# Middle periods: two turned blocks ahead of the first logits tile, its maximum behind one pass of the third sum, its exponential inside an attended tile

## The reference

```
for n in range(2):                       # STEPS
    q = Xa @ W1.T @ W2.T ; k = Xa @ W3.T
    probs  = softmax(q @ k.T)            # 2048 x 2048
    A      = probs, per row only the largest entries whose sum reaches 0.9 (top-p), renormalised
    Xf     = R @ Xf                      # R = row-normalised adj + I
    Xa     = A @ Xa
    Z      = Z + Xf @ U1[n].T + Xa @ U2[n].T
```

## Time and profile before

| | us |
|---|---|
| runs (3) | 1101.89 median, 1100.0 to 1106.16 |
| profiled execution | 1101.68 |
| its span, first to last instruction | 1099.9 |
| PE busy | 843.0 |
| DVE busy | 778.8 |
| ACT busy | 511.9 |
| POOL busy | 68.5 |
| mean granted TensorE clock | 0.890 of full speed |

### The profile page before, as it was taken

The page is one execution under the profiler, slowest core; times in us unless marked ns, Lnnn a source line. Parts: engine busy times, 40 slices in busy tenths (PEclk is TensorE's granted clock), DMA queues, the critical chain, the costliest instruction groups (busy, mean ns, idle before and its releaser), DMA issues.

```text
span 1099.9 us, 12251 instructions
## 1 busy us (share of the span) xinstructions
PE 843.0 (77%) x3886; PEld 568.4 (52%) x3886; DVE 778.8 (71%) x2357; ACT 511.9 (47%) x979; POOL 68.5 (6%) x66
## 2 busy tenths in 40 slices
PE   5889959853787778558778188688678899997695
PEld 5754326532565666456455065557575485543342
DVE  5968679799989989932788898798887102235715
ACT  4876245265466476223533835836743431123212
POOL 0120110000000000000000000000011100002201
PEclk9989988886998998979788599999788899998798
DMA  9859122420013021000134000401322467400001
GB/s 341 330 197 430 62 76 87 143 77 1 1 49 106 1 82 73 1 1 1 36 118 153 1 1 1 153 1 37 127 113 105 162 270 293 166 1 0 1 0 38
DMA packets 18734, 105.50 MB, mean 96 GB/s; under 512 B 1745, under 2 KB 7393, under 8 KB 8417
## 3 DMA queue, kind: packets, MB, share of 16 engines
q1 hardware_dynamic: 17264, 104.02, 25.4%
q10 hardware_dynamic: 1392, 0.61, 0.2%
HBM read 85.74 MB, written 18.88 MB: 95 GB/s over the span
## 4 chain that ended last, share of the span: by engine, by line
PE 42%; DVE 35%; ACT 9%; issue 9%; POOL 2%; DMA 2%; DVEq 1%; POOLq 0%; SPq 0%; ACTq 0%
DVE AT L1474 13%; PE PS L764 8%; PE PS L702 5%; PE PS L635 5%; PE PS L822 5%; DVE mxv L1613 4%; PE PS L505 4%; DVE nd L1477 3%; PE PS L1018 3%; PE PS L994 3%; DVE AT L2052 2%; PE PS L1024 2%; ACT BC L1207 2%; ACT AT L1207 2%; DVE se L1467 2%
## 5 line engine op out<-in xcount | busy, mean ns | idle before, releaser
L702 PE MATMUL PS<-K,ST 128*128 128x512 f32 x224 | 125.8, 714 | 82.2 <-ACT EA L1175 59.4
L1040 ACT ACTIVATE AT<-PS 128x512 f32<-128x512 f32 (+2 forms) x240 | 118.3, 557 | 125.2 <-PE PS L505 114.6
L702 PEld LDWEIGHTS PS<-K,ST 128*128 128x128 f32 x224 | 49.4, 232 | 143.7 <-issue 143.6
L505 PE MATMUL PS<-ident,AT 128*128 128x128 f32 x544 | 81.1, 282 | 42.7 <-DVE rS L2094 24.5
L1474 DVE SCALAR_TENSOR_TENSOR AT<-EA,se 128x2048 uint8<-128x2048 f32 (+1 forms) x46 | 107.6, 2345 | 1.9 <-DVE se L1467 0.6
L1474 DVE SCALAR_TENSOR_TENSOR AT<-AT 128x2048 uint8<-128x2048 f32 (+2 forms) x48 | 96.1, 2002 | 7.6 <-PE PS L505 6.6
L1613 DVE TENSOR_REDUCE mxv<-PS 128x1 f32<-128x2048 f32 x32 | 73.2, 2286 | 26.9 <-PE PS L702 21.4
L505 PEld LDWEIGHTS PS<-ident,AT 128*128 128x128 f32 x544 | 65.2, 145 | 51.1 <-DVE rS L2094 25.5
L2052 DVE MAX8 AT<-AT 128x8 f32<-128x256 f32 x256 | 88.4, 412 | 0.8
L764 PE MATMUL PS<-AT 128*128 128x128 f32 x512 | 70.2, 287 | 14.8 <-ACT AT L1040 14.2
L764 PEld LDWEIGHTS PS<-AT 128*128 128x128 f32 x512 | 65.1, 199 | 19.6 <-ACT AT L1040 17.7
(11 more groups left out here) (290 smaller groups left out, 1474.8 us busy)
## 6 DMA issues: line engine op xcount, KB each, us to landing
AT<-keep_at SPq DMA_DIRECT2D x32, 1024.0 KB, 5.1
EA<-in_adj SPq DMA_DIRECT2D x28, 1024.0 KB, 6.2
keep_at<-AT SPq DMA_DIRECT2D x8, 2048.0 KB, 25.0
AT<-keep_at SPq DMA_DIRECT2D x7, 2048.0 KB, 13.1
AT<-in_adj SPq DMA_DIRECT2D x4, 1024.0 KB, 10.0
EA<-keep_degrees SPq DMA_DIRECT2D x1, 1024.0 KB, 6.6
keep_x<-K SPq DMA_DIRECT2D x4, 256.0 KB, 8.5
out<-EA SPq DMA_DIRECT2D x4, 256.0 KB, 2.3
```

What stands on the lines that cost most here:

```text
L505: return pe.transpose(dst, src, ident[0:p, 0:p])
L702: mm = pe.matmul(bank(half(gi, k) + n), ST[1][:, k * P:(k + 1) * P], wide_keys[:, n * BK:(n + 1) * BK], start=True, stop=True)
L1040: return act.activation(dst, src, ACT.Copy)
```

## The change

On TensorE the logits of tile 1 move from ahead of attended tile 0 to the place of `between` in it, behind its first two turned blocks. On VectorE, in groups that are not the first of a step, the maximum of tile 1 moves from behind three passes of the third sum to behind one. On ScalarE `attend` gets a second hook, `inside`, behind the copy of the third turned block, and the exponential of tile 1 moves there from behind attended tile 0.

```
 TensorE
-                    if g > 0 and more:
-                        logits(step, g + 1, 1)
                     for k in range(G):
                         if g > 0:
-                            attend(step, g - 1, k, (lambda: logits(step, g + 1, k + 1)) if more and 0 < k < G - 1 else None)
+                            attend(step, g - 1, k, (lambda: logits(step, g + 1, k + 1)) if more and k < G - 1 else None)
 ScalarE
-            def attend(step, g, k, between=None):
+            def attend(step, g, k, between=None, inside=None):
...
                     if b == 1 and between:
                         between()
+                    if b == 2 and inside:
+                        inside()
...
-                            attend(step, g - 1, k, (lambda: guess(step, g + 1)) if more and k == G - 1 else None)
+                            attend(step, g - 1, k, (lambda: guess(step, g + 1)) if more and k == G - 1 else None,
+                                   inside=(lambda: exponential(step, g + 1, 1)) if more and k == 0 else None)
...
-                        if g > 0 and more and k < G - 1:
+                        if g > 0 and more and 0 < k < G - 1:
                             exponential(step, g + 1, k + 1)
 VectorE, third_sum
                 mass_above(E, gi, 0)
                 remember(q, 1)
+                if gi not in BOTH:
+                    between()
                 mass_above(E, gi, 1)
                 v.wait(1)
                 weigh(q)
                 mass_above(E, gi, 2)
                 v.wait(1)
                 weighed()
-                between()
+                if gi in BOTH:
+                    between()
```

## The result

The changed kernel took 1115.02 us in the median of four runs (1113.16 to 1116.43), against 1102.76 for the kernel before (four runs, 1100.0 to 1106.16): ratio 1.0109, 95% interval 1.0075 to 1.0142. The prediction was 1102.9, with 1098.5 to 1108.5 as its range: wrong. The profiled execution took 1113.16 us, its span 1111.4, so 11.5 us more span than before.

A forecast was written before the change was run, and what follows sets the result against it. No whole engine was the bound; in middle periods tile 2's exponential awaited its maximum and the scaled copy, nearly tied. 1101.68 + 0 + 0 + 0 - 0.1 + 1.3 gave 1102.9 us, range 1098.5 to 1108.5.

The forecast's parts named there:

- Steps 1 to 4, the order: Middle periods: logits 2 come 2.3 us earlier, but tile 2's exponential still waits for its unmoved maximum; at most -0.1 us.
- Step 5, the clock: TensorE's changed holes in middle periods may bring its lower clock level at logits 3; +1.3 us, out of 0 to 7.3.
- mostly the first hole take the blow: The new 1.8 to 3.9 us hole inside attended tile 0 mostly draws the lower level, hidden by 2.2 us of slack.
- 14.90 to 20.40 us row: Trace stretch with only transposes on TensorE, granted clock averaging 0.69; cited as showing that the clock rose during them.
- The rival that named it: Lower clock at logits 3 and attended tile 2 of each middle period; 1.82 us each, 7.3 in four, 1109.0; chance 0.15.
- Logits 1 too late for their maximum: VectorE's earlier maximum of tile 1 waits for logits 1, margin 0.17 us; up to 5.2 us, 1106.9; chance 0.06.
- Turned blocks and the clock: Eight transposes ahead of logits 1 can only bring the higher clock forward; sign: logits 1 below 5.4 us.

The follow-up runs named there:

- e1: Changed kernel plus 12 unused multiplications on TensorE in the hole ahead of logits 3 of each middle period; 1101.56 us, ratio 0.9999 to the kernel before.
- f1: Changed kernel with the maximum of tile 2 also moved, ahead of the first candidate pass in the middle periods; 1095.65 us, ratio 0.9938.
- e2: Changed kernel plus 6 unused multiplications in attended tile 3 of each middle period, logits 3 left as they are; 1105.34 us, ratio 1.0038.
- e6: Changed kernel plus one more VectorE pass, its sum unused, at the end of the first group of each step; 1118.8 us, ratio 1.0151.
- e5: Changed kernel plus 6 unused multiplications on TensorE ahead of logits 3 of each middle period; 1115.07 us, ratio 1.0121.
- e7: Kernel before plus one more VectorE pass, its sum unused, at the end of the first group of each step; 1110.2 us, ratio 1.0077.
- e4: Changed kernel without TensorE's part: logits 1 ahead of attended tile 0 as in the kernel before; 1115.95 us, ratio 1.0135.
- f2: Kernel before with only the maximum of tile 2 moved ahead of the first candidate pass; 1101.43 us, ratio 0.9993.

## Why the prediction was wrong

- *Steps 1 to 4, the order:* right, to 0.1 us in this period but for one size. Maximum of tile 1 at 10.87 us after the selection (354.00 - 343.10 = 10.9 forecast), attended tile 0's scaled copy at 14.70 instead of 14.15 (0.55 later, 0.3 forecast), tile 2's exponential at 27.00 with 2.33 us of idling (about 2.2). That this cancels the gain is shown by e1, which has no clock loss and equals the kernel before, and by f1, where it doesn't cancel.
- *Step 5, the clock:* this term failed. It was +1.3 us out of 0 to 7.3, and measured 13.3 in the profiled middle periods. Three things in it were wrong. First, I let "mostly the first hole take the blow": in the profile it did so in none of four periods, because logits 1 stayed slow (5.32 to 5.71 us), which left only 1.96 to 2.35 us in that hole. It does happen, in e2 and e6, but not reliably. Second, the price per stretch (1.82 at most, 1.70 measured) was right and the number of stretches was not: there are two in a period, and I had no term for the one at attended tile 3, whose hole doesn't change. Third, I judged holes by their length, by the reading that in the trace of the kernel before those up to 3.21 us were followed by full speed. That reading was false: the same trace has the lower level behind 3.01, 3.13 and 2.08 us (shown under e5), the first of them at the start of my own 14.90 to 20.40 us row. e5 and e7 add 2.61 and 2.53 us.
- *The rival that named it* (slower by the hole ahead of logits 3, 1109.0, chance 0.15) had the mechanism and the place. Its own rows, slow after 3.40 and 3.89 us, spoke for it at a hole of 3.8. It should have been the forecast; the second stretch would still have been missed.
- *Logits 1 too late for their maximum:* did not happen; VectorE's row shows no wait ahead of it.
- *Turned blocks and the clock:* I had said that the transposes ahead can only bring the higher level forward. Logits 1 took 5.33 us against 5.49, and 5.32, 5.57 and 5.71 against 5.56, 5.43 and 5.53 in the other three, so hardly. Help is seen only now and then: in e2 and e6 they took 4.36 to 4.78 us in four periods, while no kernel without the turned blocks ahead (before, e4, e7, f2) went below 5.43. In e2 and e6 these four are just the periods in which the hole inside attended tile 0 was long (2.88 to 3.31 us) and logits 3 ran at full speed. The Trainium skill ("TensorE: Matmul & The Clock Gate", Part 4: PE-mode transpose) says that transposes don't bring the higher clock as other work does. That is near to the changed kernel's logits 1, but not to the 14.90 to 20.40 us row: there only transposes ran, 32 of them, and the granted clock was 0.51 up to 18.30 and 0.98 from there on.
- The Trainium skill's advice against idle gaps of TensorE above about 3 us (same page, "Why this matters for your kernels") pointed the right way, but the runs differ from it below that: 2.53 and 2.61 us were followed by the lower level, and in the kernel before 2.08 us too, while 3.21 us was not.

What stays open: what decides beside a hole's length. The runs show that holes of one length go either way as they fall (e7 above all, and the profiles of e2 and e6), not by what rule, nor how much of it is the moment and how much what TensorE did before.

## What to carry to other kernels

When an edit leaves an engine waiting longer without moving the end, ask what that wait does to TensorE's clock: the idle time that "costs nothing" cost 12 to 13 us here, and twelve useless multiplications per period gave it back. Price such a hole as if it brought the lower level every period, at each piece of critical work behind it, and don't trust a schedule's own lucky holes: 2.35 us of other work shifted the kernel before into them. And where two releasers end within 0.1 us, an edit has to move both.

## What the runs showed of the hardware

A hole of 2.15 us, unchanged in every kernel with it, was followed by eight matmuls in 1.16 us in the kernel before and by up to 2.08 us in e7, so by either of TensorE's two levels. Slow stretches often come in company: taking away the idling ahead of logits 3 (e1) removed the one some 13 us later as well, although the hole ahead of that was left as it was. But either also comes alone: in e6's first and third period attended tile 3 is slow (2.05 and 1.91 us for its first eight matmuls) behind logits 3 at full speed, and in e2 filling the later hole left logits 3 slow. And the outcome can differ from one period to the next in one execution (e2), which is why single profiles of such kernels say less than their medians.
